# Gated cross-attention block: value products of four heads in 32-column tiles, row sums of probabilities by sets of ones

## The reference, cut to what matters

```python
scores = jnp.einsum('bhqd,bhkd->bhqk', qh, kh) / math.sqrt(hd)      # hd = 32, 16 heads
causal = ki <= qi                                                   # qi = arange(512) + 1089
scores = jnp.where(causal[None, None], scores, -10000.0)
attn = jax.nn.softmax(scores, axis=-1)
out = jnp.einsum('bhqk,bhkd->bhqd', attn, vh)
...
x = x + jnp.tanh(g_xattn[0]) * mha(layernorm(x), ctx, ctx)          # 4 x 512 x 512
x = x + jnp.tanh(g_ffn[0]) * ffn(layernorm(x), w_gate, w_up, w_down)# hidden 1408, rounded to float8
```

## Time and profile before

| | us |
|---|---|
| median of 3 runs | 1160.27 |
| lowest, highest | 1158.86, 1160.71 |
| the profiled execution: its own time | 1161.19 |
| its span (first to last instruction) | 1159.4 |
| PE busy | 970.5 (84%) |
| DVE busy | 859.7 (74%) |
| ACT busy | 656.5 (57%) |
| POOL busy | 332.1 (29%) |

### The profile page before, as it was taken

One profiled execution on the slowest core, in us unless ns is written; L12 is line 12 of the kernel. 1 busy time (PEld: TensorE's weight loads), 2 busy tenths in 40 slices (PEclk: granted clock), 3 DMA queues, 4 the chain that ended last, 5 costly groups with the idle time before them and its releaser, 6 DMA issues.

```text
span 1159.4 us, 21085 instructions
## 1 busy us (share of the span) xinstructions
PE 970.5 (84%) x7770; PEld 399.4 (34%) x7770; DVE 859.7 (74%) x1438; ACT 656.5 (57%) x1343; POOL 332.1 (29%) x350
## 2 busy tenths in 40 slices
PE   4588889888879989999889999998899999984344
PEld 2233333333323334343334333333333343432222
DVE  7768789887747888777677877787778786446764
ACT  2165567675646666666556666665566666753321
POOL 3012323332101414132323232222314132443343
PEclk9998899999989999999999999999999999996766
DMA  7942423230572221114812121218421110000000
GB/s 147 154 122 69 115 66 93 66 86 26 112 88 57 66 57 39 53 43 83 124 41 60 63 61 36 51 41 115 70 61 35 27 41 10 2 10 10 10 10 19
DMA packets 155119, 70.69 MB, mean 61 GB/s; under 512 B 111032, under 2 KB 142856, under 8 KB 155016
## 3 DMA queue, kind: packets, MB, share of 16 engines
q1 hardware_dynamic: 153256, 63.57, 26.5%
q0 software_dynamic: 1760, 5.77, 1.8%
HBM read 39.08 MB, written 4.19 MB: 37 GB/s over the span
## 4 chain that ended last, share of the span: by engine, by line
PE 42%; DVE 36%; issue 10%; ACT 4%; POOL 4%; DMA 2%; SPq 1%; POOLq 0%; DVEq 0%; ACTq 0%
DVE mch L1069 17%; PE ps L866 13%; PE ps L842 8%; PE ps L887 6%; PE ps L780 5%; PE ps L910 3%; DVE ff L985 2%; DVE ff L981 2%; DVE ff L989 2%; PE ps L785 2%; ACT pr L632 1%; DVE upd L1112 1%; DMA qst<-mrow 1%; PE ps L848 1%; DVE cmb L1102 1%
## 5 line engine op out<-in xcount | busy, mean ns | idle before, releaser
L632 ACT ACTIVATE pr<-ps 128x512 f32<-128x512 f32 (+4 forms) x832 | 397.2, 530 | 250.0 <-PE ps L842 125.1
L1069 DVE TENSOR_REDUCE mch<-ps 128x2 f32<-128x1024 f32 (+4 forms) x416 | 432.3, 1056 | 69.2 <-PE ps L780 32.8
L866 PE MATMUL ps<-pr,vf 128*33 128x512 f32 (+4 forms) x1664 | 380.6, 537 | 0.0
L842 PE MATMUL ps<-qst,kst 97*64 97x512 f16 (+4 forms) x1600 | 250.5, 371 | 18.0 <-DMA qst<-mrow 11.4
L780 PE MATMUL ps<-kTh,qTh 32*128 32x512 f16 (+4 forms) x832 | 156.2, 373 | 59.2 <-DVE mch L1069 40.7
L780 PEld LDWEIGHTS ps<-kTh,qTh 32*128 32x128 f16 x832 | 39.5, 92 | 279.0 <-DVE mch L1069 106.9
L842 PEld LDWEIGHTS ps<-qst,kst 97*64 97x64 f16 (+1 forms) x1600 | 77.3, 111 | 108.0 <-ACT pr L632 57.4
L866 PEld LDWEIGHTS ps<-pr,vf 128*33 128x33 f32 (+1 forms) x1664 | 86.8, 113 | 56.6 <-issue 4.9
L1141 DVE SCALAR_TENSOR_TENSOR ff<-ps,scs,wsb 128x352 f32<-128x352 f32 x56 | 32.6, 583 | 73.1 <-PE ps L887 73.1
L448 POOL TENSOR_TENSOR t_q<-ff 128x768 bf16<-128x768 f32 (+1 forms) x28 | 47.4, 1694 | 100.1 <-DVE ff L989 100.1
L887 PE MATMUL ps<-wgu,t_T 128*64 128x352 bf16 x768 | 66.5, 316 | 0.0
(11 more groups left out here) (151 smaller groups left out, 1198.2 us busy)
## 6 DMA issues: line engine op xcount, KB each, us to landing
kst<-kTh SPq DMA_DIRECT2D x128, 100.1 KB, 2.2
ksrc<-in_ctx SPq DMA_DIRECT2D x16, 768.0 KB
vf<-in_ctx SPq DMA_DIRECT2D x48, 256.0 KB, 5.1
kst<-kTl SPq DMA_DIRECT2D x64, 100.1 KB, 2.2
xs<-in_x SPq DMA_DIRECT2D x16, 256.0 KB, 4.8
qst<-qTh SPq DMA_DIRECT2D x128, 32.0 KB, 1.9
out<-xs SPq DMA_DIRECT2D x16, 256.0 KB, 2.0
ff<-in_L_ffn_w_down SPq DMA_DIRECT2D x4, 704.0 KB, 4.4
```

What stands on the lines that cost most here:

```text
L632: nc.scalar.activation(pr[0:kn, n % NP, q0:S], ps[0:kn, j, q0:S], ACT.Exp, scale=SCALE).then_inc(ex_done, 1)
L842: last = nc.tensor.matmul(ps[a:e, j, q0:S], kst[s][0:ST, r, k0 + a:k0 + e], qst[s][0:ST, r, q0:S], start=True, stop=(t < DT))
L866: nc.tensor.matmul(ps[64 * j:64 * j + VW, 2 + pp % 2, q0:S], vf[0:kn, t, h, :], pr[0:kn, n % NP, q0:S], start=(t == 0), stop=(t == NT - 1) ...
L1069: nc.vector.tensor_reduce(mch[:, qt, 2 * hp:2 * hp + 2, c], both[:, :, 0:k1 - k0], AX.X, ALU.max).then_inc(dve_free, 1)
```

## The change

Five things are changed together.

1. **Order of heads.** A step is now key tile `t = u // 2` and pair `i = u % 2`: head pairs alternate.
2. **Value products.** Once in two steps (steps 3, 5, ... 27) the products of all four heads for one key tile go to the four 32-partition quarters of one PSUM bank. There is no column of ones any more, and `vf` loses its 33rd column.
3. **Row sums.** POOL adds the probabilities of each odd key tile to those of the even tile before it, in place (`join_probs`: 12 adds in a group, 1024 float32 a partition in the first eight, then 898 and 386). PE then multiplies the even tiles by a 128x32 block of ones, four heads at once, into a second bank (`prob_sums`, 7 in a group). The ring of probabilities is now two slots for even tiles and three half-slots for odd ones.
4. **End of a group.** One `out_copy`, one `sums_copy`, one `out_turn` (four transposes and four matmuls of 4 columns), one `join_out` and one `add_update` for four heads, at step 4 of the next group.
5. **Tiles and room.** Scores, masks on scores, masked sums and both feed-forward products go in quarters of 32 columns instead of halves of 64. `kTl` and `qTl` have one buffer instead of two, so that DVE waits for the transfers of the group before; `put_heads` is one call of 24 transfers and stands behind `put_shift` and the value loads; the scratch of software DMA is 2048.

```diff
+    QUARTERS = tuple((P // 4 * i, P // 4 * (i + 1)) for i in range(4))
+    EVEN, ODD = (NT + 1) // 2, NT // 2
+    EVEN_SLOTS, ODD_SLOTS = 2, 3
...
+    def values_at(at):
+        gg, u = divmod(at - 3, STEPS)
+        return (gg, u // 2) if u % 2 == 0 and 0 <= gg < GALL else None
+    def joined_at(at):
+        gg, u = divmod(at - 4, STEPS)
+        m, i = divmod(u, 4)
+        return (gg, m, i) if i < PAIRS and m < ODD and 0 <= gg < GALL else None
+    def added_at(at):
+        gg, u = divmod(at, STEPS)
+        if u in (0, 2):
+            return (gg - 1, ODD - 1 + u // 2) if 1 <= gg <= GALL else None
+        m, rest = divmod(u - 8, 4)
+        return (gg, m) if rest == 0 and 0 <= m < ODD - 1 and gg < GALL else None
...
-        vf = sb("vf", [P, NT, H, VW])
+        vf = sb("vf", [P, NT, H, HD])
-        pr = sb("pr", [P, NP, S])
-        oT = sb("oT", [P, S])
+        pr = sb("pr", [P, PAIRS * EVEN_SLOTS + ODD_SLOTS, 2, S])
+        oT, oS = sb("oT", [P, S]), sb("oS", [P, S])
...
+        def join_probs(pool, gg, m, i):
+            q0 = Q0[2 * m + 1]
+            pool.wait_ge(pv_done, value_count(gg, 2 * m))
+            pool.wait_ge(ex_done, exp_count(gg, 2 * m + 1, i))
+            even, odd = ((EVEN * gg + m) % EVEN_SLOTS) * PAIRS + i, PAIRS * EVEN_SLOTS + (PAIRS * (ODD * gg + m) + i) % ODD_SLOTS
+            nc.gpsimd.tensor_tensor(pr[:, even, :, q0:S], pr[:, even, :, q0:S], pr[:, odd, :, q0:S], ALU.add).then_inc(pair_joined, 1)
...
-            for j in range(2):
-                n, h = unit(gg, u, j), g * GH + 2 * i + j
-                pe.wait_ge(ex_done, n + 1)
-                nc.tensor.matmul(ps[64 * j:64 * j + VW, 2 + pp % 2, q0:S], vf[0:kn, t, h, :], pr[0:kn, n % NP, q0:S],
-                                 start=(t == 0), stop=(t == NT - 1)).then_inc(pv_done, 1)
+            pe.wait_ge(ex_done, exp_count(gg, t, PAIRS - 1))
+            for r in range(GH):
+                last = nc.tensor.matmul(ps[HD * r:HD * (r + 1), 2, q0:S], vf[0:kn, t, g * GH + r, :], prob(gg, t, r)[0:kn, q0:S],
+                                        start=(t == 0), stop=(t == NT - 1))
+            last.then_inc(pv_done, 1)
+
+        def prob_sums(pe, gg, m):
+            t = 2 * m
+            kn, q0 = KT[t][1], Q0[t]
+            if m == 0 and gg >= 1:
+                pe.wait_ge(sums_ev, gg)
+            if m < ODD:
+                pe.wait_ge(pair_joined, join_count(gg, m, PAIRS - 1))
+            for r in range(GH):
+                last = nc.tensor.matmul(ps[HD * r:HD * (r + 1), 3, q0:S], onesf[0:kn, 0:HD], prob(gg, t, r)[0:kn, q0:S],
+                                        start=(m == 0), stop=(m == EVEN - 1))
+            last.then_inc(sums_done, 1)
...
+            if gg >= 1 and part == PARTS[0]:
+                for r in range(GH):
+                    dve.wait_ge(stk[(gg - 1) % 2][r], ((gg - 1) // 2 + 1) * STK)
...
-        nc.vector.memset(ps[:, 2:4, :], 0.0).then_inc(ps_clear, 1)
```

More of the change, by code:

```diff
@@ L357, in _ @@
             sp.wait_ge(dve_free, dve_count["stage", 0, 0])
-            for i in range(PAIRS):
-                put_heads(sp, 0, i)
+            put_heads(sp, 0)
             for t in range(3, NT):
@@ L366, in _ @@
             sp.wait_ge(dve_free, dve_count["stage", 1, 0])
-            for i in range(PAIRS):
-                put_heads(sp, 1, i)
+            put_heads(sp, 1)
             for gg in range(GALL):
@@ L815, in suffix_turn, with out_turn @@
             last.then_inc(suf_mm, 1)
-        def out_turn(pe, pp):
-            job = ("turn", pp)
+        def out_turn(pe, gg):
+            job = ("turn", gg)
             free_slot(pe, job)
-            pe.wait_ge(o_ev, pp + 1)
-            n = 64 + VW
+            pe.wait_ge(o_ev, gg + 1)
             for qt in range(QT):
-                last = nc.tensor.transpose(slot(job)[:, qt * n:(qt + 1) * n], oT[0:n, qt * P:(qt + 1) * P], idf[0:n, 0:n])
+                nc.tensor.transpose(slot(job)[:, qt * P:(qt + 1) * P], oT[:, qt * P:(qt + 1) * P], idf[:, :])
+            pe.wait_ge(sums_ev, gg + 1)
+            for qt in range(QT):
+                last = nc.tensor.matmul(slot(job)[:, S + GH * qt:S + GH * (qt + 1)], oS[:, qt * P:(qt + 1) * P],
+                                        idf[:, :].rearrange("p (h d) -> p h d", h=GH)[:, :, 0], start=True, stop=True)
             last.then_inc(o_tr, 1)
         def scores(pe, gg, u):
-            i, t = divmod(u, NT)
+            t, i = divmod(u, PAIRS)
             k0, kn = KT[t]
@@ L840, in scores @@
                     pe.wait_ge(ex_done, n - 1)
-                for a, e in halves:
+                quarters = [(a, min(e, kn)) for a, e in QUARTERS if a < kn]
+                for a, e in quarters:
                     last = nc.tensor.matmul(ps[a:e, j, q0:S], kst[s][0:ST, r, k0 + a:k0 + e], qst[s][0:ST, r, q0:S],
@@ L952, in _ @@
                     scores(pe, gg, u)
-                if LAG <= at < LAST + LAG:
-                    values(pe, (at - LAG) // STEPS, (at - LAG) % STEPS)
+                if values_at(at) is not None:
+                    values(pe, *values_at(at))
                 for n, k in tiles_at(at):
@@ L1058, in stage_low @@
             dve.wait_ge(hi_done, 3 * gg + PARTS.index(part) + 1)
+            if gg >= 1 and part == PARTS[0]:
+                for r in range(GH):
+                    dve.wait_ge(stk[(gg - 1) % 2][r], ((gg - 1) // 2 + 1) * STK)
             hi, lo = ((qTh, qTl), (kTh, kTl), (kTh, kTl))[part]
-            nc.vector.tensor_tensor(lo[:, gg % 2, c0:c1], slot(("stage", gg, part))[:, 0:c1 - c0], hi[:, gg % 2, c0:c1],
+            nc.vector.tensor_tensor(lo[:, c0:c1], slot(("stage", gg, part))[:, 0:c1 - c0], hi[:, gg % 2, c0:c1],
                                     ALU.subtract).then_inc(dve_free, 1)
@@ L1088, in suffix_weigh, with join_out @@
                                     ALU.mult).then_inc(dve_free, 1)
-        def join_out(dve, s, pp):
-            gg, i = divmod(pp, PAIRS)
-            k, n = gg % 2, 64 + VW
-            got = slot(("turn", pp))[:, 0:QT * n].rearrange("p (t n) -> p t n", t=QT)
-            sums = [got[:, :, HD + 64 * j] for j in range(2)]
-            dve.wait_ge(o_tr, pp + 1)
+        def join_out(dve, s, gg):
+            got = slot(("turn", gg))
+            update = upd[:, :, :, :].rearrange("p t h d -> p (t h d)")
+            heads = upd[:, :, :, :].rearrange("p t h d -> p (t h) d")
+            dve.wait_ge(o_tr, gg + 1)
@@ L1096, in join_out @@
             dve.wait_ge(cw_ready, gg + 1)
             dve.wait_ge(dve_free, dve_count["suf", gg])
-            for j in range(2):
-                s.step(nc.vector.tensor_tensor(den[:, 0, :, j], cw[:, k, :, 2 * i + j], sums[j], ALU.add))
-            for j in range(2):
-                h = 2 * i + j
-                ins = nc.vector.tensor_tensor(cmb[:, :, j, :], got[:, :, 64 * j:64 * j + HD], sw[:, :, h * HD:(h + 1) * HD], ALU.add)
-                if j == 0:
-                    s.step(ins)
-            s.settle()
@@ new lines, in join_out @@
+            if gg >= 1:
+                dve.wait_ge(xs_done, gg)
+            s.step(nc.vector.tensor_tensor(update, got[:, 0:S], sw[:, :, :].rearrange("p t n -> p (t n)"), ALU.add))
+            s.settle()
+            nc.vector.reciprocal(den[:, 1, :, :], den[:, 0, :, :]).then_inc(dve_free, 1)
+            dve.wait_ge(dve_free, dve_count["turn", gg])
+            nc.vector.scalar_tensor_tensor(heads, heads, tg[:, 0:1],
+                                           den[:, 1, :, :].rearrange("p t h -> p (t h)").unsqueeze(2).broadcast_to([P, QT * GH, HD]),
```

171 lines of the change are left out of this document (88 added, 83 removed).

## The result

The changed kernel takes 1328.39 us (1327.65 to 1329.41, 4 runs) against 1160.49 us of the kernel before on the same chip: a ratio of 1.145, 95% interval 1.143 to 1.147. The forecast had the sign (slower) and was 148 us short, far outside its range.

The account below looks back on a forecast made before the run. It took PE and DVE in turn to bound the kernel. 1161.2 - 24 (PE) - 11 (joins) - 1 (PSUM clearing) - 15 (transfers) + 72 (adds holding DVE) = 1182, less 0.9 is 1181; it said 1180 us, range 1092 to 1228.

Parts of the forecast that it names:

- The adds themselves: POOL's adds of probabilities: 2.35, 2.09 and 1.01 us for 1024, 898 and 386 columns, 400 us in all.
- The lock: DVE instructions with two SBUF inputs or in two-port mode wait for the rest of a POOL add: +72 us, ends 15 and 135.
- who is exposed: DVE instructions said to meet adds: 78 in weight jobs (37 us) and 96 in feed-forward tiles (45 us), before weighting.
- an add that was held off by one DVE instruction can slip in ahead of the next: Upper end of the wait per exposed DVE instruction: 0.9 us, since such an add costs its whole 2.35 us.
- the price of a held microsecond: Share of DVE's held time counted as kernel time: 82% in weight jobs (30 us), 93% in feed-forward tiles (42 us).
- rival 3: Row sums on PE wait for late POOL adds, holding ACT and DVE behind: 48 us more, 1228 us; chance 0.08.
- PE's part: Values and sums on PE fall to 289 us, 91 us less; of it -24 us counted, ends 12 and 91.
- The join: DVE's joins at the end of a group: 16 of 1.85 us for 32 of 1.28 us, -11 us.
- Order of the pairs: Alternating head pairs, charged only within PE's work: wide scores again add 0.4 us in steps 12 to 14.
- Transfers: Packed value rows load in one piece and waits for the shift row shrink: -15 us, ends 5 and 20.
- Rival 1: POOL and DVE seldom meet (15 us) and PE gets back half of its 91 us: 1090 to 1157 us; chance 0.37.
- Rival 4: PE's instruction count becomes the bound (1280 us), or four column tiles don't run together (over 1500 us); chance 0.04 together.

Follow-up runs that it names:

- the kernels with useless work: Useless POOL products added that no other engine waits for: kernel before 1229.83 us; changed kernel with one-column adds and two odd slots 1271.65 us.
- the kernel with tiny adds: Changed kernel with each of POOL's 192 adds of probabilities cut to one column, leaving out nearly all odd key tiles from the row sums: 1170.14 us.
- the useless matmuls: Four zero-weight matmuls in ten steps a group where PE idles: changed kernel with one-column adds 1178.84 us; with full adds, step 20's waiting for the shift, 1261.91 us.
- the two kernels of 1170 us: Changed kernel with adds of one column, 1170.14 us, and changed kernel without adds, with seven sets of row sums a group, 1170.78 us.
- the kernel with full adds and the end of the maxima first: Changed kernel with all adds, whose add of step 20 waits on POOL for the next group's shift, the result of max_finish: 1277.42 us.
- the kernel with seven sums and no adds: Changed kernel without any add on POOL, seven sets of row sums a group, odd key tiles left out: 1170.78 us.

## Why the prediction was wrong

The sum was 1181 us by the medians, and 1328 came: 147 us. 1109 us of it stood for the kernel without the adds' price, where 1171 was measured (62 us), and 72 us for the adds, where 158 were (86 us).

*The adds themselves* were right: 405.5 us for 400, 2.13 us each for 2.35, 2.09 and 1.01 mixed, POOL 735.7 us for 730.

*The lock* was the right mechanism: the products of the kernels with useless work show it with no data between the engines. Two steps of this term failed.

The first is the list "who is exposed". It left out `max_finish` and `join_out`, which end in DVE instructions with two SBUF inputs or a `tensor_scalar`: the last two of the first grew from 8.5 us to 41.9 us, and keeping adds off them gave 51 us back. It is the worst place that a run tested: two short dependent instructions, each of which is held in 10 or more of 16 groups by an add, at a step where two adds stand, and no maxima go on until they are through. The clause "an add that was held off by one DVE instruction can slip in ahead of the next" comes near, but here the second add was not held off; it followed the first at once. The instructions that were on the list were costed too high. Against the kernel with tiny adds the three lines of the weight jobs and roundings took 41.5 us more and line 1149 took 13.9 more, 55 us for 82. The rest of DVE's 102 us are 33 in `max_finish`, 6 in `join_out` and 7 in the two small products behind the layer norms (L1115 and L1121).

The second is the price of a held microsecond, and it weighs more. The sum took 0.82 to 0.93. The 102 us by which DVE's busy time exceeds that of the kernel with tiny adds cost 158, so 1.5 each. At the sum's own price the 102 us would have cost 90, 18 more than forecast; the other 68 of the 86 us are the price. One part is the lateness of the sums, 30 us, put into rival 3 with a chance of 0.08 as though it excluded the lock: it is the lock's companion. Another is the clock, 0.81 to 0.92, of which the useless matmuls gave back 15 us. The three parts, 51, 30 and 15, were not measured together, and the rest, the holds of the listed instructions, was not taken away by any run.

In the structure's 62 us several steps failed, and no run takes them wholly apart.

*PE's part*, 24 us, can't be called right. Values and sums take 323.0 us without adds, 57.6 less than before where 91 was forecast; values took 210.2 us for half of 380.6, sums 112.8 for 99. Times 0.44 that is 25 us, but two errors cancel in it, less work saved and more worth each. And PE's whole busy time fell by only 15.4 us, from 970.5 to 955.1, as other work grew: scores take 266.8 us for 250.5. At 0.78 or less that is 12 us at most. The scores in quarters were costed at nothing; but halves are no faster in the changed kernel (275.4 us for 277.1), so their growth is not shown to come from the quarters.

*The join* was relieved as said (its instructions keep DVE busy for 28.3 us where they took 38.8, overlaps counted once), but the products of line 1149 take 46.8 us for 37.3 without any adds, as in the new order ten of them begin while POOL adds value sums (L525), where none did before. DVE's busy time is 858.0 us for 859.7, and the 11 us never came.

*Order of the pairs* was charged only inside PE's part; with the moved transfers it costs 16 us, of which the same line 1149 has a share (43.7 us there). *Transfers* gave 7 or 8 us for 15, if that. Together these are about 12 + 10 + 16 + 7 = 45 of the 62 us, with overlaps among the first three; some 17 us of the structure or more stay open. One candidate was looked at: the granted clock from 60 to 250 us is 0.84 to 0.87 in the two kernels of 1170 us, for 0.96 before. Useless matmuls raised it by 0.02 there and gained nothing, which does not settle it.

*Rival 1* had its own test in the text, whether line 1149 and its like keep their durations; they did not (1286 ns for 776). *Rival 4* is out: four column tiles run together, and quarters cost less than halves.

## What to carry to other kernels

Before work is put on POOL, list every DVE instruction that can be held by it, the shortest first, and look at which of them the others wait behind: two dependent instructions of 0.17 us in each group cost DVE more here (33 us) than the 48 products of line 1149 (14). A wait that keeps the long POOL instruction off such a place (one condition here, 51 us) was worth more than shorter instructions (14 us), which hold less each but come late in sum. And measure what a microsecond of an engine's work is worth by taking away some of it at two sizes, before a gain is counted, and count work the same way on both sides: here it was 0.44 by the line that was cut and 0.72 to 0.78 by PE's whole busy time.

## What the runs showed of the hardware

- Two adds of 898 columns held two DVE instructions of 16 columns, each until the add that it met had ended, 1.41 and 2.00 us for 0.17, and left a reduction in the same place alone (0.22 us). This agrees with the Trainium skill, SBUF — State Buffer, section "Who interferes with whom", and shows the cost to the short and dependent ones. Useless products on a buffer of their own do the same in the kernel before (on average 1.21 us for the first of the two instructions, and 1.24 for one of 256 columns that took 0.49).
- POOL's in-place product with both inputs in one place took 1.69 us where the add of two buffers took 2.13, by the same shapes. Operation and operands differ both, so which of them matters is not shown.
- Four column tiles of 32 run together: eight float32 matmuls of 512 columns for four heads took 0.86 us to the start of the next work, where four of them for two heads took 0.96.
- Useless matmuls in the kernel with full adds and the end of the maxima first raised the granted clock from 0.83 to 0.88 and from 0.86 to 0.93 in two stretches, and the kernel took 15 us less. Yet two runs of the kernel with seven sums and no adds had mean clocks of 0.897 and 0.925 at the same time (1171.06 and 1170.50 us): a mean clock alone doesn't tell the time.
